# A recommendation tower on one core: layer 1 beside the next unit's first dots, layer 2 half a cycle on, the last unit's first tile in layer 1 ahead of the last rows

## The chip, the core and the metric

The kernel runs on one core of a Trainium2 chip. Time is device microseconds of one execution. The engines are TensorE (PE), VectorE (DVE), ScalarE (ACT), GpSimd (POOL) and SyncE (SP). Each works through its own list of instructions in order, and they wait for each other by semaphores only. DMAs are issued by SP, POOL and, at the end, ACT.

## What is computed

A batch of 2048 samples has one dense vector and 26 embeddings, gathered from 26 tables, all of 128 floats. The 351 dot products of all pairs of these 27 vectors, joined with the dense vector, go through three layers.

```python
e = jnp.stack([tbl_0[ids[:, 0]], ..., tbl_25[ids[:, 25]]], axis=1)   # 2048 x 26 x 128
T = concatenate([r_dense[:, None, :], e], axis=1)                   # 27 vectors of each sample
z = einsum('bnd,bmd->bnm', T, T)[:, iu0, iu1]                       # pairs n < m: 351
h = concatenate([z, r_dense], axis=1)                               # 479
h = maximum(h @ W_top1 + b_top1, 0.0)                               # 512
h = maximum(h @ W_top2 + b_top2, 0.0)                               # 256
y = h @ W_top3                                                      # 1
```

All of it is float32.

## The kernel before

The batch is cut into 16 tiles of 128 samples; two tiles (l = 0 and 1) are a unit, so there are 8 units u, and END is 7. Every sample needs its 27 vectors in `T`, with the 128 features on the partitions. They come in two ways.

*Rows.* 16 of the embeddings are gathered by GpSimd (`gather`, L420), one indirect DMA for each tile and table, into `rows[:, l]`. With the dense vector they make five rounds (`turn`, r = 0 to 4, with 3, 4, 4, 3 and 3 vectors). TensorE transposes a round into a bank of `look_ps` (`turn`, L743), and ScalarE copies it into `T` (`turn_out`, L600). `gather` of tile t waits until the same round of tile t - 2 has been turned.

*Lookups.* The 10 tables with 1000 rows are looked up by matrix products. VectorE compares ids with row numbers into `hot` (`compare`, L455), TensorE multiplies `hot` with the table, cut into a high part `tab_hi` and a low part `tab_lo` (`look`, L733), and ScalarE copies out (`look_out`, L588 or L592). The split of a table is VectorE's `split` (L440, L443) and ScalarE's `hi_out` (L568). Three tables, named WHOLE (1, 3 and 5), are split during unit 0's loop; their raw copies lie in the buffers that `w1` (chunks 0 and 1), `pairs` and `h1` use later, and the scratch of their split lies in `w2`. There are six lookup groups for a unit.

*Dots.* `products(u, l, b)` (L759) multiplies `T` with itself, 128 instructions for a tile. VectorE copies them to `gram` (`gram_out`, L479). For a unit SyncE stores `gram` in DRAM (`dots`, 4 DMAs, L337) and loads it back as `pairs`, in three chunks with pairs on the partitions (L342 and L343).

*Layers.* `layer1(u, ...)` (L779) has 16 products with 256 columns: for each of four output chunks f three chunks of `pairs` and one of the dense part. ScalarE's `h1_out` (L615) is bias and relu, eight instructions in two halves. `layer2(u)` (L789) has 8 products, VectorE's `y_out` (L489, L493) is the rest. The last unit goes tile by tile, with half the columns: `last_layer1(l)` (L800), `last_h1_out` (L622), `last_layer2` (L822), `last_y_out` (L498, L500). Its stores and loads are `shuffle_last` on SP and `last_store`, `last_load` on ACT.

The order on every engine is written out by hand. One turn of TensorE's loop for unit u is, in this order: turn(u,1,0), layer 2 of unit u-2, dots of tile (u,0), turn(u,1,1), lookup group 0 of unit u+1, turn(u,1,2), group 1, turn(u,1,3) and (u,1,4), group 2, half of layer 1 of unit u-1, turn(u+1,0,0), the other half, dots of tile (u,1), turn(u+1,0,1), group 3, turn(u+1,0,2) and (u+1,0,3), group 4, turn(u+1,0,4), group 5. At the end, after the loop: turn(END,1,0), layer 2 of unit 5, dots of (END,0), turn 1, layer 1 of unit 6 with turns 2 and 3 in between, turn 4, layer 2 of unit 6, dots of (END,1), then `last_layer1(0)`, `last_layer2(0)`, `last_layer1(1)`, `last_layer2(1)`. `look_ps` has four banks, taken in turn by turns and lookup groups.

SyncE's loop loads the dense vectors and the ids (`load_ids_near`) of later units, then calls `shuffle(u)`. In unit 0 it also loads the weights of layer 1, in many small pieces (L322): chunk 2 first, chunk 0 (9 pieces) when table 1 is split, chunk 1 (13 pieces) after the loads of the pairs, and then `w2`. All weights and biases count on one semaphore, `weights_landed`.

Of the kernel before, what the change touches and what calls it, by code (L numbers as in the profile page):

```python
# [63 lines left out]
def dlrm_tower(nc, r_dense, ids, tables, W1, b1, W2, b2, W3, out):  # L64
# [36 lines left out]
    WEIGHTS = 16 * (len(w1_pieces) + 5)  # L101
# [4 lines left out]
    with ExitStack() as ctx:  # L106
# [59 lines left out]
        weights_landed = sem("weights_landed")  # L166
# [92 lines left out]
        def l1_order(u):  # L259

            return (2, 3, 0, 1) if u == END - 1 else (0, 1, 2, 3)

        def last_l1(l, f):
            if l == 0:
                return look_ps[:, f // 2, f % 2 * P:(f % 2 + 1) * P]
            return [mlp_ps[:, 0, 0], mlp_ps[:, 1, 0], gram_ps[:, 0], gram_ps[:, 1]][f][:, 0:P]
# [31 lines left out]
        def _(sp):  # L299
# [19 lines left out]
            def load_pair_weights(c):  # L319
                for w_row, cnt, chunk, r, step in w1_pieces:  # L320
                    if chunk == c:
                        sp.dma_start(w1[r:r + step * (cnt - 1) + 1:step, c, :], W1[w_row:w_row + cnt, :]  # L322
                                     ).then_inc(weights_landed, 16)

            def load_small_weights():
                sp.dma_start(w1[:, PC, :], W1[PAIRS:PAIRS + D, :]).then_inc(weights_landed, 16)
                with nc.allow_non_contiguous_dma(reason="a few hundred words"):
                    sp.dma_start(bias1[:], b1.rearrange("(c p) -> p c", p=P)).then_inc(weights_landed, 16)
                sp.dma_start(w3[:], W3.rearrange("f o -> o f").to_broadcast([P, F2])).then_inc(weights_landed, 16)
                sp.dma_start(bias2[:], b2.rearrange("(o f) -> o f", o=1).to_broadcast([P, F2])).then_inc(weights_landed, 16)  # L330

            def shuffle(u):
# [3 lines left out]
                for j in range(NJ):  # L336
                    sp.dma_start(*dots_store(dots[u % 2], j, 0, 2 * NI)).then_inc(dots_stored, 16)  # L337
                if u >= 2:
# [36 lines left out]
            for u in range(END):  # L375
# [4 lines left out]
                if u == 0:  # L380
# [3 lines left out]
                    sp.wait_ge(lo_ready, split_count(WHOLE[1]))  # L384
                shuffle(u)
# [43 lines left out]
        def _(dve):  # L429
# [53 lines left out]
            def y_out(u):  # L483

                if u == 0:
                    dve.wait_ge(weights_landed, WEIGHTS)
# [43 lines left out]
            for u in range(END):  # L530
# [3 lines left out]
                if u > 1:  # L534
                    y_out(u - 2)
# [6 lines left out]
                gram_out(u, 1)  # L542
                if u == 0:
# [12 lines left out]
            y_out(END - 2)  # L556
            dense_out(END, 1)
            gram_out(END, 1)
            y_out(END - 1)
# [4 lines left out]
        def _(act):  # L564
# [39 lines left out]
            def h1_out(u, half):  # L604
                if u == 0 and half == 0:
                    act.wait_ge(weights_landed, WEIGHTS)
# [3 lines left out]
                for f in l1_order(u)[half * F1C // 2:(half + 1) * F1C // 2]:  # L610
# [7 lines left out]
            def last_h1_out(l):  # L618
                for step in range(F1C if l else F1C // 2):
                    act.wait_ge(l1_done, 2 * END + 2 * l + step + 1)  # L620
                    for f in ([step] if l else [2 * step, 2 * step + 1]):
# [45 lines left out]
            for u in range(END):  # L667
                turn_out(u, 1, 0)
                turn_out(u, 1, 1)
                look_out(u + 1, 0)  # L670
# [8 lines left out]
                if u > 0:  # L679
                    h1_out(u - 1, 0)  # L680
                    h1_out(u - 1, 1)
# [3 lines left out]
                look_out(u + 1, 3)  # L685
                if u == 0:
                    hi_out(WHOLE[1])
                turn_out(u + 1, 0, 2)
# [8 lines left out]
            h1_out(END - 1, 0)  # L697
            turn_out(END, 1, 2)
            turn_out(END, 1, 3)
            h1_out(END - 1, 1)  # L700
            turn_out(END, 1, 4)
            last_store(range(NJ // 2, NJ))
            last_h1_out(0)
# [4 lines left out]
        def _(pe):  # L708
# [54 lines left out]
            def layer1(u, first, end):  # L763
                for i in range(first, end):
                    f, c = l1_order(u)[i // (PC + 1)], i % (PC + 1)
                    if i == 0:
                        if u == 0:
                            pe.wait_ge(weights_landed, WEIGHTS)
# [160 lines left out]
```

## Time and profile before

| | us |
|---|---|
| median of 3 runs | 368.12 |
| lowest, highest | 367.59, 368.23 |
| the profiled execution | 367.97 |
| its span, from the first to the last instruction | 366.2 |

| engine | busy us | share of the span |
|---|---|---|
| TensorE, matmul | 343.0 | 94% |
| TensorE, weight load | 320.5 | 88% |
| VectorE | 221.5 | 60% |
| ScalarE | 172.3 | 47% |
| GpSimd | 256.3 | 70% |

### The profile page before, as it was taken

The numbers are of one execution on the slowest core, as the hardware profiler recorded it, in microseconds if no ns is written. First come the engines' busy times: TensorE is split into PE (matmuls) and PEld (weight loads), VectorE is DVE, ScalarE is ACT, GpSimd is POOL, SyncE is SP. The second block draws the span as 40 slices with busy tenths as digits, with TensorE's granted clock in tenths as the row PEclk, the third lists the DMA queues.
The fourth block names the chain that finished last, engine by engine and source line by source line (L and its number), as shares of the span: only waits on it lengthen the run. The fifth ranks groups of instructions, "written<-read, shape, count | busy, mean of one in ns | idle before, by whom it ended". The sixth has DMA issues, their size and how long they took to land.

```text
span 366.2 us, 9895 instructions
## 1 busy us (share of the span) xinstructions
PE 343.0 (94%) x4042; PEld 320.5 (88%) x4042; DVE 221.5 (60%) x786; ACT 172.3 (47%) x220; POOL 256.3 (70%) x263
## 2 busy tenths in 40 slices
PE   3997899879699999999999999999999999999976
PEld 2887798769689999999989999999989998999766
DVE  3989968886436677375936576466936484613231
ACT  5266738543356345561556244563556253344211
POOL 6787777777777777777777777777777777775000
PEclk9999999999899999999999999999999999999998
DMA  7996232355325622255215622363225322454030
GB/s 208 268 260 179 62 124 77 86 146 166 104 56 119 177 62 57 70 132 162 59 52 134 167 63 58 78 154 124 60 59 134 98 59 52 99 133 86 21 57 6
DMA packets 45878, 39.07 MB, mean 107 GB/s; under 512 B 32930, under 2 KB 39113, under 8 KB 45834
## 3 DMA queue, kind: packets, MB, share of 16 engines
q1 hardware_dynamic: 36014, 21.40, 22.1%
q0 software_dynamic: 8192, 16.79, 17.7%
q8 instruction: 32, 0.52, 0.6%
q10 hardware_dynamic: 1628, 0.25, 0.5%
q14 instruction: 12, 0.10, 0.1%
HBM read 32.40 MB, written 6.02 MB: 105 GB/s over the span
## 4 chain that ended last, share of the span: by engine, by line
PE 82%; DVE 4%; POOL 4%; DMA 4%; issue 3%; ACT 1%; ACTq 0%; SPq 0%; DVEq 0%
PE look_ps L733 35%; PE gram_ps L759 14%; PE mlp_ps L779 13%; PE look_ps L743 7%; PE mlp_ps L789 7%; POOL rows L420 4%; PE look_ps L724 4%; DVE hot L455 3%; DMA rows<-in_tbl_dram,ids_all 1%; DMA dots_last<-gram 1%; DMA ids_all<-in_ids_dram 1%; DMA pairs<-dots_last 1%; PE mlp_ps L800 1%; PE gram_ps L800 1%; PE look_ps L822 1%
## 5 line engine op out<-in xcount | busy, mean ns | idle before, releaser
L420 POOL DMA_INDIRECT rows<-in_tbl_dram,ids_all x240 | 237.6, 990 | 73.2 <-issue 71.0
L455 DVE TENSOR_SCALAR hot<-ids_near 125x256 fp32r<-125x256 f16 x640 | 148.4, 302 | 43.2 <-PE look_ps L733 34.5
L733 PE MATMUL look_ps<-hot,tab_hi 125*128 125x256 f32 x616 | 155.5, 292 | 5.8 <-ACT tab_hi L568 2.9
L733 PE MATMUL look_ps<-hot,tab_lo 125*128 125x256 f32 x616 | 151.1, 284 | 0.0
L733 PEld LDWEIGHTS look_ps<-hot,tab_hi 125*128 125x128 f32 x616 | 118.6, 192 | 7.4 <-issue 5.3
L600 ACT COPY T<-look_ps 128x384 f32<-128x384 f32 (+1 forms) x80 | 85.4, 1113 | 71.6 <-PE look_ps L743 71.6
L733 PEld LDWEIGHTS look_ps<-hot,tab_lo 125*128 125x128 f32 x616 | 118.8, 193 | 0.1
L479 DVE COPY gram<-gram_ps 128x432 f32<-128x432 f32 x64 | 38.8, 607 | 68.9 <-PE gram_ps L759 56.2
L592 ACT COPY T<-look_ps 128x512 f32<-128x512 f32 x32 | 38.6, 1206 | 75.3 <-PE look_ps L733 75.3
L759 PEld LDWEIGHTS gram_ps<-T 128*54 128x54 f32 x2048 | 53.9, 130 | 8.5 <-issue 4.5
L759 PE MATMUL gram_ps<-T 128*54 128x54 f32 x2048 | 57.4, 214 | 2.1 <-DVE gram L479 1.0
L743 PE MATMUL look_ps<-ident,rows 128*128 128x128 f32 x272 | 41.5, 276 | 3.2 <-DMA rows<-in_tbl_dram,ids_all 1.8
L779 PE MATMUL mlp_ps<-pairs,w 117*128 117x256 f32 x168 | 40.9, 379 | 0.0
L743 PEld LDWEIGHTS look_ps<-ident,rows 128*128 128x128 f32 x272 | 31.1, 141 | 5.6 <-DMA rows<-in_tbl_dram,ids_all 2.1
L779 PEld LDWEIGHTS mlp_ps<-pairs,w 117*128 117x128 f32 x168 | 30.7, 189 | 3.7
L789 PE MATMUL mlp_ps<-w,h 128*128 128x256 f32 x112 | 25.4, 380 | 0.9 <-ACT h L615 0.9
L789 PEld LDWEIGHTS mlp_ps<-w,h 128*128 128x128 f32 x112 | 20.7, 190 | 3.7 <-ACT h L615 1.1
L615 ACT ACTIVATE h<-mlp_ps,bias 128x128 f32<-128x128 f32 x56 | 16.0, 382 | 12.9 <-PE mlp_ps L779 12.9
L420 POOL DMA_INDIRECT rows<-in_tbl_dram,ids_first x16 | 17.9, 1117 | 5.8 <-issue 4.6
L577 ACT ACTIVATE ids_near<-ids_near,minus_row 125x2560 f16<-125x2560 f16 x7 | 17.0, 2435 | 0.7 <-DMA ids_near<-ids_rows 0.7
L779 PE MATMUL mlp_ps<-dense,w 128*128 128x256 f32 x56 | 16.7, 379 | 0.0
L588 ACT COPY T<-look_ps 128x256 f32<-128x256 f32 x16 | 11.5, 719 | 5.8 <-PE look_ps L733 5.8
(72 smaller groups left out, 133.6 us busy)
## 6 DMA issues: line engine op xcount, KB each, us to landing
dots<-gram SPq DMA_DIRECT2D x28, 182.2 KB
ids_near<-ids_rows SPq DMA_DIRECT2D x7, 640.0 KB, 6.3
rows<-in_tbl_dram,ids_all POOLq DMA_INDIRECT x240, 2.6
T<-in_tbl_dram SPq DMA_DIRECT2D x5, 448.0 KB
pairs<-dots SPq DMA_DIRECT2D x14, 117.0 KB
rows<-in_r_dense_dram SPq DMA_DIRECT2D x16, 64.0 KB
gram<-in_tbl_dram SPq DMA_DIRECT2D x2, 448.0 KB
pairs<-dots SPq DMA_DIRECT2D x7, 104.0 KB
```

Of the source, the lines that this page charges most:

```text
L420: pool.indirect_dma_start(rows[:, t % 2, place[n], :], None, tables[n - 1], bass.IndirectOffsetOnAxis(ap=index[:, n - 1:n].bitcast(U32), a ...
L455: eq = nc.vector.tensor_scalar(hot[:VP, at % 2, c], ids_near[:VP, u % 2, k], float(c), None, ALU.is_equal)
L479: nc.vector.tensor_copy(gram[:, :, :, first:first + PER], gram_ps[:, b % 2, 0:2 * PER * NV].rearrange("p (i s n) -> p s n i", s=2, n=NV)). ...
L577: nc.scalar.activation(ids_near[:VP, u % 2], ids_near[:VP, u % 2], ACT.Identity, bias=minus_row[:VP]).then_inc(ids_relative, K)
L592: nc.scalar.copy(T_unit(u)[:, :, :, n0:n1 + 1:n1 - n0].rearrange("p l q n -> p n l q"), src.rearrange("p (n l q) -> p n l q", n=2, l=2)).t ...
L600: nc.scalar.copy(T_tile(u, l)[:, :, n:n + cnt].rearrange("p q n -> p n q"), look_ps[:, bank_of(("turn", u, l, r)), 0:cnt * P].rearrange("p ...
L615: relu = nc.scalar.activation(by_sample[:, g], by_pair[:, g], ACT.Relu, bias=bias1[:, f:f + 1])
L733: mm = pe.matmul(dst, w[:VP, k, c], hot[:VP, slot, c], start=(c == 0 and half == 0), stop=(c == CH - 1 and half == 1))
L743: mm = pe.transpose(look_ps[:, bank, i * P:(i + 1) * P], rows[:, l, place[n], :], ident[:])
L759: mm = pe.matmul(gram_ps[64 * g:64 * g + 2 * NV, b % 2, at:at + 2 * NV], src[:, g, i], src[:, g, i], start=True, stop=True)
L779: mm = pe.matmul(mlp_ps[:, f * 2 // F1C, f % 2], w1[:kk, c, f * P:(f + 1) * P], rhs, start=(c == 0), stop=(c == PC))
L789: mm = pe.matmul(mlp_ps[:, 0, l], h1[:, c, l * P:(l + 1) * P], w2[:, c], start=(c == 0), stop=(c == F1C - 1))
```

## The change

SyncE's `shuffle(u)` is cut into `store_dots(u)` and `load_pairs(u)`. In unit 0 weight chunk 1 is issued right behind chunk 0, ahead of the stores, and `w2` between the stores and the loads of the pairs. `weights_landed` becomes three semaphores: `w1_landed`, `w2_landed` and `small_landed` (dense part of W1, biases, W3).

On TensorE layer 1 is cut into `layer1_dense(u)`, the dense products of output chunks 0 and 2, and `layer1_pairs(u)`, the other 14. In the loop `layer1_dense(u-1)` stands ahead of the dots of tile (u,0), where layer 2 of unit u-2 stood, and `layer1_pairs(u-1)` behind turn(u,1,1). `layer2(u-1)` stands where the second half of layer 1 stood, behind turn(u+1,0,0). At the end `layer2(END-1)` and then `last_layer1(0)` stand ahead of turn(END,1,4) and of the last dots, and `last_layer1(0)` writes to one bank of `mlp_ps`. ScalarE's `h1_out` goes behind turn_out(u,1,1), `hi_out(3)` goes ahead of look_out(1,3), and `last_h1_out(0)` goes ahead of `last_store`. VectorE's `y_out(u-1)` goes behind `gram_out(u,1)`, where `y_out(u-2)` stood further ahead.

```diff
@@ SyncE
+                    load_pair_weights(1)
+                store_dots(u)
                 if u == 0:
-                    load_pair_weights(1)
                     sp.wait_ge(hi_ready, K)
                     sp.wait_ge(lo_ready, K)
-                    sp.dma_start(w2[:], W2.rearrange("(c p) f -> p c f", p=P)).then_inc(weights_landed, 16)
+                    sp.dma_start(w2[:], W2.rearrange("(c p) f -> p c f", p=P)).then_inc(w2_landed, 16)
+                load_pairs(u)
...
@@ VectorE
-                if u > 1:
-                    y_out(u - 2)
                 dense_out(u, 1)
...
                 gram_out(u, 1)
+                if u > 0:
+                    y_out(u - 1)
...
@@ ScalarE
                 turn_out(u, 1, 1)
+                if u > 0:
+                    h1_out(u - 1, 0)
+                    h1_out(u - 1, 1)
                 look_out(u + 1, 0)
...
                 turn_out(u + 1, 0, 1)
+                if u == 0:
+                    hi_out(WHOLE[1])
                 look_out(u + 1, 3)
-                if u == 0:
-                    hi_out(WHOLE[1])
...
             turn_out(END, 1, 4)
+            last_h1_out(0)
             last_store(range(NJ // 2, NJ))
-            last_h1_out(0)
...
@@ TensorE
+            def layer1_dense(u):
+
+                if u == 0:
+                    pe.wait_ge(small_landed, SMALL_LANDED)
+                pe.wait_ge(dense_ready, 2 * u + 2)
+                if u > 0:
+
+                    pe.wait_ge(y_ready, 2 * u)
+                    pe.wait_ge(h1_ready, F1C * u)
+                for f in range(0, F1C, 2):
+                    layer1_begin(u, f)
+
+            def layer1_pairs(u):
+                if u == 0:
+                    pe.wait_ge(w1_landed, W1_LANDED)
+                pe.wait_ge(shuffled[u % 2], SHUFFLED * (u // 2 + 1))
...
                 turn(u, 1, 0)
-                if u > 1:
-                    layer2(u - 2)
+                if u > 0:
+                    layer1_dense(u - 1)
                 for b in range(BLOCKS):
                     products(u, 0, b)
                 turn(u, 1, 1)
+                if u > 0:
+                    layer1_pairs(u - 1)
...
-                if u > 0:
-                    layer1(u - 1, 0, 8)
                 turn(u + 1, 0, 0)
                 if u > 0:
-                    layer1(u - 1, 8, 16)
+                    layer2(u - 1)
...
             turn(END, 1, 3)
...
+            layer2(END - 1)
+            last_layer1(0)
             turn(END, 1, 4)
-            layer2(END - 1)
             for b in range(BLOCKS):
                 products(END, 1, b)
-            last_layer1(0)
             last_layer2(0)
```

## Rows read from the trace of the kernel before

**Rows 1.** The page's part 1: busy us, share of the span, instructions.

```profile
PE 343.0 (94%) x4042; PEld 320.5 (88%) x4042; DVE 221.5 (60%) x786; ACT 172.3 (47%) x220; POOL 256.3 (70%) x263
```

**Rows 2.** Timeline of GpSimd, the last gather: start us, us, what, idle before.

```profile
335.02 0.94 POOL L420 DMA_INDIRECT rows<-in_tbl_dram,ids_all  x1 [0.31 <-issue]
```

**Rows 3.** Chain of waits in unit 2's loop: start us, us, what.

```profile
152.25 0.58 PE look_ps L743 x4
152.84 3.84 PE look_ps L733 x32
...
161.92 3.46 PE mlp_ps L789 x16
```

**Rows 4.** Timeline of TensorE, start of unit 1, rows with idle time before them.

```profile
71.68 0.36 PE L733 MATMUL look_ps<-hot,tab_hi 125*128 125x256 f32 x1 [1.56 <-ACT tab_hi L568]
...
75.42 0.35 PE L733 MATMUL look_ps<-hot,tab_hi 125*128 125x256 f32 x1 [1.27 <-DVE hot L455]
...
82.98 0.66 PE L743 MATMUL look_ps<-ident,rows 128*128 128x128 f32 x4 [0.43 <-DMA rows<-in_tbl_dram,ids_all]
```

**Rows 5.** Chain of waits, unit 1, ahead of and behind its last turn.

```profile
88.77 4.35 DMA rows<-in_tbl_dram,ids_all
...
93.66 1.46 issue
...
95.72 5.25 PE look_ps L733 x32
```

**Rows 6.** Windows: A:B, length, busy PE PEld DVE ACT POOL, granted clock, DMA share, GB/s.

```profile
95.10:101.00 5.90, 5.88 (x36) 5.90 (x37) 2.11 (x9) 0.92 (x1) 4.51 (x5) 0.71 0.24 65
...
358.20:361.40 3.20, 3.20 (x17) 3.20 (x16) 0.00 (x0) 1.15 (x4) 0.00 (x0) 0.51 0.00 0
```

**Rows 7.** Timeline of VectorE around the split of the last table.

```profile
68.89 1.82 DVE L455 TENSOR_SCALAR hot<-ids_near 125x256 fp32r<-125x256 f16 x8
71.63 0.69 DVE L440 TENSOR_SCALAR w<-h 125x1024 int32<-125x1024 int32 x1 [0.92 <-ACT tab_hi L568]
```

**Rows 8.** Timeline of SyncE's queue, DMA issues: start us, us of issuing, line.

```profile
60.64 3.80 SPq L322 DMA_DIRECT2D w<-in_W_top_dram  x9
69.00 5.43 SPq L337 DMA_DIRECT2D dots<-gram  x4
77.38 2.24 SPq L342 DMA_DIRECT2D pairs<-dots  x3
79.66 0.48 SPq L343 DMA_DIRECT2D pairs<-dots  x1
80.18 6.78 SPq L322 DMA_DIRECT2D w<-in_W_top_dram  x13
...
164.71 0.48 SPq L343 DMA_DIRECT2D pairs<-dots  x1
```

**Rows 9.** Chain of waits from the last unit's first dots to the end.

```profile
324.34 3.46 PE mlp_ps L789 x16
...
337.87 1.75 PE mlp_ps L779 x8
...
340.84 3.72 PE mlp_ps L789 x16
344.56 3.49 PE gram_ps L759 x128
...
354.50 2.44 DMA pairs<-dots_last
...
361.34 1.96 PE look_ps L822 x8
```

**Rows 10.** Timeline of VectorE behind the second tile's dots, unit 2.

```profile
154.86 3.89 DVE L455 TENSOR_SCALAR hot<-ids_near 125x256 fp32r<-125x256 f16 x16 [1.95 <-PE look_ps L733]
```

**Rows 11.** Timeline of TensorE behind the last dots, the start of last_layer2(0).

```profile
351.63 0.69 PE L822 MATMUL look_ps<-w,h 128*128 128x256 f32 x2
```

**Rows 12.** Timeline of ScalarE, a turn's copy near the end.

```profile
337.91 0.91 ACT L600 COPY T<-look_ps 128x384 f32<-128x384 f32 x1 [0.27 <-PE look_ps L743]
```

More of the change, by code:

```diff
@@ L555, in _ @@
             gram_out(END, 0)
-            y_out(END - 2)
+            y_out(END - 1)
             dense_out(END, 1)
             gram_out(END, 1)
-            y_out(END - 1)
             last_y_out(0)
@@ L609, in h1_out @@
                     act.wait_ge(l2_done, u)
-                for f in l1_order(u)[half * F1C // 2:(half + 1) * F1C // 2]:
+                for f in range(half * F1C // 2, (half + 1) * F1C // 2):
                     by_sample = h1[:, f].rearrange("p (l g i s) -> p g s l i", l=2, g=2, s=2)
@@ L618, in last_h1_out @@
             def last_h1_out(l):
-                for step in range(F1C if l else F1C // 2):
-                    act.wait_ge(l1_done, 2 * END + 2 * l + step + 1)
-                    for f in ([step] if l else [2 * step, 2 * step + 1]):
+                for step in range(F1C if l else 1):
+                    act.wait_ge(l1_done, 2 * END + l + step + 1)
+                    for f in ([step] if l else range(F1C)):
                         nc.scalar.activation(h1[:, f, l * P:(l + 1) * P].rearrange("p (g i s) -> p g s i", g=2, s=2),
@@ L684, in _ @@
                 turn_out(u + 1, 0, 1)
-                look_out(u + 1, 3)
                 if u == 0:
                     hi_out(WHOLE[1])
+                look_out(u + 1, 3)
                 turn_out(u + 1, 0, 2)
@@ L761, in products, with layer1_begin @@
                 mm.then_inc(gram_done, 1)
[L763 to L766, printed above, removed]
-                        if u == 0:
-                            pe.wait_ge(weights_landed, WEIGHTS)
-                        pe.wait_ge(shuffled[u % 2], SHUFFLED * (u // 2 + 1))
-                        pe.wait_ge(dense_ready, 2 * u + 2)
-                    if u > 0 and c == 0 and f == 0:
-                        pe.wait_ge(y_ready, 2 * u)
-                    if u > 0 and c == 0 and f == 2:
-                        pe.wait_ge(h1_ready, F1C * u)
-                    kk = P if c == PC else KP
-                    rhs = dense[:, u % 2] if c == PC else pairs[:kk, u % 2, c]
-                    mm = pe.matmul(mlp_ps[:, f * 2 // F1C, f % 2], w1[:kk, c, f * P:(f + 1) * P], rhs,
-                                   start=(c == 0), stop=(c == PC))
-                    if c == PC and f % 2 == 1:
+            def layer1_begin(u, f):
+                pe.matmul(mlp_ps[:, f * 2 // F1C, f % 2], w1[:, PC, f * P:(f + 1) * P], dense[:, u % 2],
+                          start=True, stop=False)
+            def layer1_dense(u):
[11 more added lines that the diff above has]
+                pe.wait_ge(shuffled[u % 2], SHUFFLED * (u // 2 + 1))
+                for f in range(F1C):
+                    if f % 2 == 1:
+                        layer1_begin(u, f)
+                    for c in range(PC):
+                        mm = pe.matmul(mlp_ps[:, f * 2 // F1C, f % 2], w1[:KP, c, f * P:(f + 1) * P],
+                                       pairs[:KP, u % 2, c], start=False, stop=(c == PC - 1))
+                    if f % 2 == 1:
                         mm.then_inc(l1_done, 1)
             def layer2(u):
+                if u == 0:
+                    pe.wait_ge(w2_landed, W2_LANDED)
                 pe.wait_ge(h1_ready, F1C * (u + 1))
```

45 lines of the change are left out of this document (20 added, 25 removed).

## The prediction

> **What bounds the kernel now.** I read five views. The page's busy shares come first [rows 1]: TensorE is busy 343.0 of 366.2 us and GpSimd, with its gathers, 256.3 us. The latter figure understates GpSimd, because between two gathers it always pauses 0.30 us. Its last gather starts at 335.02 and ends at 335.96 [rows 2], 256 gathers of some 1.3 us end to end. So two engines run through side by side with no reserve to speak of. The chain of waits says which of them ends last. From 95.7 us to 339.6 us it stays on TensorE without a hole, with a period of 40.6 us per unit. [Rows 3] are three pieces of it: the dots of the second tile of unit 2 end at 152.25, a lookup group of 32 instructions takes 3.84, and the 8 products of layer 2 at 161.92 take 3.46; layer 1 has 16 products of the same width. In that stretch an order on TensorE costs nothing and brings nothing as long as no wait appears or goes. What an order can change lies in two places: the start of unit 1 (70 to 101 us), where TensorE waits, and the end (after 324 us).
>
> In the start, the timeline of TensorE shows waits of 1.56 us for ScalarE's `tab_hi`, of 1.27 us for VectorE's `hot` and of 0.43 us for gathered rows [rows 4]; the chain then has 1.46 us more ahead of the last `turn`, and after that 32 lookup instructions take 5.25 us [rows 5] instead of 3.84. The granted clock tells why: 0.71 over 95.1 to 101 and 0.51 over 358.2 to 361.4 [rows 6], which is a stretch at the 1.2 GHz level (full busy time; 5.9 x 0.29 / 0.5 = 3.4 us of it in the first), each time after TensorE had been largely idle. Such a stretch under full work costs half its length, 1.7 us.
>
> **The start, step by step.** Three edits meet here.
>
> (a) ScalarE makes `hi_out` of whole table 3 ahead of `look_out(1, 3)`. VectorE's `hot` for that table ends at 68.89 + 1.82 = 70.71, and its next split began only at 71.63 because it waited 0.92 us for `tab_hi` [rows 7]. With the copy made first, lookup group 4 starts at 70.8 in place of 71.68 and the chain behind (split, `hot`, lookup group 5 at 75.42) comes 0.9 us earlier: `turn(1,1,0)` ends at about 76.8 in place of 77.7.
>
> (b) SyncE issues the 13 pieces of weight chunk 1 ahead of the stores of the dots and the big `w2` load ahead of the loads of the pairs. The old order is in [rows 8]: 9 pieces until 60.64 + 3.80 = 64.44, stores 69.00 to 74.43, pair loads 77.38 to 80.14, 13 pieces in 6.78 us after that. The new one: pieces 64.4 to 71.2, stores 71.2 to 76.7, `w2` one issue (about 0.5), landed stores 2.95 us after their last issue, as before (74.43 to 77.38), so 79.6; pair loads issued 79.6 to 82.4. A pair load took 2.44 us from issue to the matmul that uses it [rows 9]; the last one, issued at 81.9, is there at 84.4 on quiet queues. With `w2` and gathers in flight I take 85.0. The bounds are 84.0 and 86.3 (4.35 us, the gathered rows that came late in the same traffic [rows 5]).
>
> (c) TensorE now has 2 dense products (2 of the 8 in 3.46 us [rows 3], 0.87) ahead of the dots of unit 1, and 14 products (6.05 us) right behind `turn(1,1,1)`. Dots at 77.7 + 3.5 = 81.2; that turn waited for its rows until 82.98 [rows 4], which land perhaps 0.5 earlier with less traffic; it ends at 83.1. The products wait for the pairs until 85.0: a new wait of 1.9 us, bounds 0.9 and 3.2. Behind it, on TensorE's queue, stand everything of units 1 and 2, so nothing covers it. They end at 91.05. Then three lookup groups (3 x 3.84), the turns (1.43) and layer 2 (3.46) make 16.4, so the dots of the second tile start at 107.5 against 108.2 before, with layer 2 of unit 0 already done. The old waits at 93 and 95 us are gone, since the rows are long there. But TensorE is idle from 81.2 with one 0.6 us turn between until 85.0, 3.2 us in all, which is like the idle ahead of 95 us and more than the 2.5 us ahead of 358 us [rows 6, 9]. I take it that the 1.2 GHz stretch comes again, at the same 1.7 us: 109.1, that is +0.9. Without it -0.8.
>
> **The steady units.** Layer 1 moves 11 to 14 us earlier, layer 2 half a unit. Their instructions are the same 16 + 8 products, so TensorE's period stays. VectorE's `y_out` (three short operations) goes between the last copy of the dots and a `hot` that waits for a lookup anyway: VectorE idles there for 1.95 us in unit 2 [rows 10], and in the others as long. I take it as hidden; without that hole it would delay lookup group 4 by at most its own length. ScalarE's eight relus now stand ahead of a `look_out` whose lookup takes 3.84 us; they take 2.3. What gets near is the pairs: the dots of a unit end, and layer 1 of it starts 9.67 us (152.25 to 161.92) + 0.87 + 3.5 + 0.59 = 14.6 us later, at 166.9 in unit 2. The last pair load is issued at 164.71 and is there at 164.71 + 2.44 = 167.15, or 0.4 later with traffic [rows 3, 8, 9]. Unit 2 has the latest of these loads (its stores took longest), unit 5 the next; the others issue about a microsecond sooner. I take 0.3 us in all, bounds 0 and 1.5. GpSimd sees all this only through `turned` of two tiles back, some 30 us of reserve, and keeps its pace. The turns of the second and third row rounds come later, that of round 1 earlier by 2.6 us; its rows have been there long enough for that in the trace.
>
> **The end.** Before, from 324.34: layer 2, dots, turn, layer 1 with turns, a wait of 340.84 - 339.62 = 1.22 us for the relus, layer 2 for 3.72, dots at 344.56 [rows 9]. After: 2 products 0.87, dots 3.53, turn 0.59, 14 products 6.05 (335.38), two turns beside the relus' 1.22 (336.6), layer 2 3.72 (340.3), then the 16 half-width products of `last_layer1(0)`. Before, they ran at 348.05 to 351.63 [rows 11], in the shadow of the store and load of the last dots (until 356.94), for nothing. Now they lie ahead of the last turn and cost 3.46: 343.8. Their pairs are not late: dots at 328.74 instead of 331.33, so landed some 2.6 earlier, at about 339.5. Then the turn 0.33, and ScalarE's copy of it 0.91 [rows 12], which layer 2 used to cover and nothing does now: dots at 345.1 against 344.56, +0.55. The last rows are no excuse to hide the 3.46 behind: they are gathered by 335.96 [rows 2] and there by about 338.5, while TensorE now arrives at 343.8.
>
> The tail after these dots (copy, store, load, 12 products, layer 2, `last_y_out`) has the same steps. I take it as before, 21.6 us, half-clock stretch included.
>
> **Sum.** 366.2 + 0.9 + 0.3 + 0.55 = 367.95 as span; on the profiled execution's 367.97 that is 369.7. The median is 0.15 above that execution: 369.9.
>
> **The rivals.** (1) The clock holds at 85 us, because a turn falls into the idle time: -1.7, 368.2. For: a wait of 1.56 and one of 1.27 us at 70 to 75 us left the clock at 1.00. Against: the idle here is 3.2 us in 3.8.
> (2) Faster. The pairs of unit 0 are there when TensorE arrives, so that neither the 1.9 us wait nor the slow stretch exists: 369.9 - 3.6 = 366.3. It decides if the last pair load lands by 83.1 us. For it: the old store took from 69.00 and nothing says that the 13 weight pieces hold it up for all of 2.2 us. Against: the issue order and 0.5 us per issue [rows 8].
> (3) Slower still. TensorE now runs out of work ahead of the tail: with `last_layer1(0)` gone from there it is idle from about 351.5 to 357.5, against 2.5 us before. The 1.2 GHz level then holds from the first of the 12 products. At 2.4 GHz these would take 2.6 us and layer 2 1.73; before, they took 4.4 (356.94 to 361.34) and 1.96 [rows 9]. All at half, 5.2 + 3.5 = 8.7, is +2.4: 372.3. The Trainium skill, TensorE: Matmul & The Clock Gate, section Part 1: The HAM clock gate, says that the throttled level is the default and only activity releases it; by that rule a longer idle ahead of the tail is never free. The trace of before agrees as far as it goes (0.51 after 2.5 us idle). How late in the tail the level comes back no row here shows.
> (4) The order has no effect beyond the two ends and the gains and losses there cancel: the start brings 0.8 (rival 1 in small) and the end takes it: 368.1.
>
> **Chances.** Forecast 0.40 (own range 369.0 to 370.8), rival 1 0.24, rival 2 0.15, rival 3 0.12, rival 4 0.09. A difference of 0.2% (0.74 us) is about what a measurement of this kernel can tell from none. Slower (above 368.9): nearly all of the forecast and rival 3, and a sixth of rival 1: 0.55. Faster (under 367.4): rival 2 and some of rival 1: 0.20. Same: 0.25. The range goes from rival 2 with little to spare to just short of rival 3: 366.5 to 371.9.
>
> **What the new profile would show.** Right: a wait of TensorE for the DMA of the pairs of unit 0 at 83 to 85 us; a granted clock of 0.5 soon after; the second dots of unit 1 at 109 us; a pair wait of some tenths near 167; `last_layer1(0)` at 340 to 344 and the last dots at about 346.7. Wrong: dots of unit 1 before 107 us (rival 2), no clock under 1.00 before the tail (rival 1), the 12 last products over 5 us (rival 3), or repeated pair waits of a microsecond in the steady units, which would put the time above the range.

## The result: 1 to 2% slower, and the profile after

| | before | after |
|---|---|---|
| median, us | 368.12 (7 runs, 367.56 to 369.40) | 373.46 (7 runs, 370.47 to 379.87) |
| the profiled execution, us | 367.97 | 377.54 |
| its span, us | 366.2 | 375.7 |

The ratio is 1.0108 with a 95% interval of 1.0078 to 1.0139. Ratios, here and below, leave out executions over 1.5% above the fastest of their kernel (of the changed kernel the three longest, 376.3 to 379.9 us, with the profiled one among them); medians leave out none. On a second chip the same kernel gave 376.45 us against 367.51, ratio 1.0226 (1.0189 to 1.0264), and the profile taken there (span 376.2) has waits of the same kinds. That one, at 377.99 us, is the longest of its six. So I read both profiles, take no size from one alone, and keep in mind that both show more than the median execution lost (9.5 us of span in the first, where the medians differ by 5.3). The forecast was 369.9 us with a range of 366.5 to 371.9. Its sign held, its size and range did not.

The page after, parts 1, 2 (granted clock) and 4:

```profile
PE 345.9 (92%) x4042; PEld 322.3 (86%) x4042; DVE 222.7 (59%) x786; ACT 171.4 (46%) x220; POOL 258.9 (69%) x263
...
PEclk9999999996999999999999999999999999999988
...
PE 73%; DMA 10%; SPq 8%; ACT 4%; DVE 2%; issue 1%; ACTq 0%; DVEq 0%
```

TensorE has the same 4042 matmul instructions as in [rows 1] and 2.9 us more busy time; the same instructions last longer where the clock is low. New in the chain of waits are 8% on SyncE's queue and 10% on DMAs: the chain now runs through the stores and loads of the dots, where before it stayed on TensorE from unit 1 to the last unit. Here are its pieces at the start (start us, us, what):

```profile
84.50 3.42 DMA pairs<-dots
88.06 2.90 PE mlp_ps L788 x6
...
95.78 1.30 PE mlp_ps L788 x6
...
113.50 3.49 PE gram_ps L760 x128
```

The first products with pairs (line 788) start at 88.06, when the last pair load of unit 0 has landed. The first group of six takes 2.90 us and the last 1.30. The dots of the second tile of unit 1 start at 113.50. The same chain further on, in the loop's unit 2 (pairs of unit 1), in its unit 5 (pairs of unit 4), and at the end:

```profile
128.33 4.28 DMA pairs<-dots
132.65 1.56 PE mlp_ps L788 x6
...
251.50 3.99 DMA pairs<-dots
...
319.54 3.46 PE gram_ps L760 x128
...
349.09 3.57 PE mlp_ps L811 x32
...
353.02 0.92 ACT T L601
...
353.99 3.56 PE gram_ps L760 x128
...
363.93 2.40 DMA pairs<-dots_last
```

Two rows of the kernel before are wanted beside these, the dots of the second tile of unit 1 and of unit 6:

```profile
108.22 3.46 PE gram_ps L759 x128
...
311.20 1.90 PE gram_ps L759 x65
```

With the last dots at 344.56 [rows 9] they cut the loss of the two profiled executions into parts. The second column is the trace after, the third that from the second chip (113.41, 318.36 and 354.50 there):

| | before | after | after, second chip |
|---|---|---|---|
| start of the dots of tile (1,1) | 108.22 | +5.3 | +5.2 |
| from there to those of (6,1) | 202.98 | +3.1 | +2.0 |
| from there to the last dots | 33.36 | +1.1 | +2.8 |
| from there to the end of the span | 21.6 | +0.1 | +0.1 |

### The profile page after: what moved, and what is told of

The parts are those of the page before. It is cut to its first block, busy times and chain, and to the rows that moved or that the text cites. A ratio compares the mean times of both kernels' runs of the same rounds, so it can differ in the third digit from the quotient of the medians.

```text
span 375.7 us, 9896 instructions
## 1 busy us (share of the span) xinstructions
PE 345.9 (92%) x4042; PEld 322.3 (86%) x4042; DVE 222.7 (59%) x786; ACT 171.4 (46%) x220; POOL 258.9 (69%) x263
## 4 chain that ended last, share of the span: by engine, by line
PE 73%; DMA 10%; SPq 8%; ACT 4%; DVE 2%; issue 1%; ACTq 0%; DVEq 0%
PE look_ps L734 31%; PE gram_ps L760 11%; PE mlp_ps L788 11%; PE mlp_ps L800 7%; PE look_ps L744 6%; DMA dots<-gram 4%; PE look_ps L725 4%; DMA pairs<-dots 3%; SPq L337 3%; PE mlp_ps L765 3%; SPq L322 3%; SPq L344 2%; DMA w<-in_tbl_dram 2%; PE mlp_ps L811 2%; DVE gram L481 1%
## 5 line engine op out<-in xcount | busy, mean ns | idle before, releaser
L422 POOL DMA_INDIRECT rows<-in_tbl_dram,ids_all x240 | 240.2, 1001 | 73.2 <-issue 69.2
L734 PEld LDWEIGHTS look_ps<-hot,tab_hi 125*128 125x128 f32 x616 | 117.2, 190 | 6.8 <-ACT T L589 2.3
L734 PEld LDWEIGHTS look_ps<-hot,tab_lo 125*128 125x128 f32 x616 | 117.5, 191 | 0.2
L788 PE MATMUL mlp_ps<-pairs,w 117*128 117x256 f32 x168 | 42.4, 397 | 4.5 <-DMA pairs<-dots 4.5
L788 PEld LDWEIGHTS mlp_ps<-pairs,w 117*128 117x128 f32 x168 | 32.9, 199 | 10.0 <-issue 3.2
```

The source lines that it names most:

```text
L422: pool.indirect_dma_start(rows[:, t % 2, place[n], :], None, tables[n - 1], bass.IndirectOffsetOnAxis(ap=index[:, n - 1:n].bitcast(U32), a ...
L734: mm = pe.matmul(dst, w[:VP, k, c], hot[:VP, slot, c], start=(c == 0 and half == 0), stop=(c == CH - 1 and half == 1))
L788: mm = pe.matmul(mlp_ps[:, f * 2 // F1C, f % 2], w1[:KP, c, f * P:(f + 1) * P], pairs[:KP, u % 2, c], start=False, stop=(c == PC - 1))
```

## What was open, and two ways of reading it

Theory A, which is the prediction's with larger sizes: TensorE waits for the pairs of unit 0 and loses its clock by that, meets late pairs again in some later units, and has `last_layer1(0)` uncovered at the end. Theory C is its rival: the new sequence of blocks costs something in itself, so that moving the wait away brings nothing back. Inside theory A it was open whether the idle time makes the clock fall, and what makes the pairs late.

## Experiments: taking the parts back

Every ratio is to the kernel before, run beside it on the same chip. The first run is the changed kernel itself (`f1_after`).

> The changed kernel on another chip than the runs before it, where every kernel took some 515 us or more because TensorE waited for its own instructions. Here I expect about 368 us for the kernel before and a ratio of 1.006 to 1.014. Theory A: wait for the pairs of unit 0 of 2 to 3.5 us, a clock of 0.5 behind it, waits of a microsecond in all for later pairs, last dots 9 us later than in the kernel before or less if the clock holds.

It gave 376.45 us, 1.0226, more than the 1.006 to 1.014 expected. Its wait for the pairs of unit 0 is 2.3 us, those of later units 1.6 us. The waits of TensorE in that trace (engine, line, what it waited for: us in total, times, longest):

```profile
PE mlp_ps L811 <- DMA pairs<-dots_last: 6.1, 1, 6.1
PE mlp_ps L788 <- DMA pairs<-dots: 3.9, 3, 2.3
```

**The products with pairs one lookup group back.**

```diff
                 turn(u, 1, 1)
-                if u > 0:
-                    layer1_pairs(u - 1)
                 look(u + 1, 0)
+                if u > 0:
+                    layer1_pairs(u - 1)
```

ScalarE's two `h1_out` go behind `look_out(u + 1, 0)` in the same way.

> The 14 products with pairs one lookup group (3.84 us) further back. Theory A: no wait for pairs from unit 0 to 5, the slow stretch at 88 us gone: 3 to 6 us less than the changed kernel, ratio to before 0.997 to 1.003. Theory C (it is the sequence of blocks on TensorE and not the waits): ratio as that of the changed kernel.

369.96 us, 1.0070 (1.0044 to 1.0096), 6.5 us under the changed kernel on the same chip. In its trace TensorE has no wait at line 788 at all, and the chain reads:

```profile
106.70 3.46 PE gram_ps L760 x128
...
310.62 3.46 PE gram_ps L760 x128
...
344.67 3.56 PE gram_ps L760 x128
```

The dots of tile (1,1) are 1.5 us earlier than before the change, not 5 later, and from there to (6,1) it takes 203.9 us where the changed kernel took 206.0 and, on this chip, 205.0. The same instructions in almost the same sequence, 3.84 us later in each unit, give 6.5 us back: theory C falls. The ratio stays above the 0.997 to 1.003 that was expected. The profiled execution, at 368.11 us the fastest of the six, is level with the trace of before: 1.5 us less at the start, 0.9 more up to the dots of (6,1), 0.7 more from there to the last dots. What makes the median 2.4 us longer than the kernel before (369.96 against 367.51) no trace shows.

**Unit 0 alone.** The same edit for u = 1 only, that is for the pairs of unit 0.

> The changed kernel with the pairs' products of unit 0 alone one lookup group back, on such a chip. Theory A: the loss at the start (2.3 to 3.0 us of wait, 3.0 of slow clock) goes, the waits of the later units stay: 369 to 372 us, ratio 1.005 to 1.012, between the changed kernel (1.023) and the one with all units moved (1.007).

370.36 us, 1.0076 (1.0048 to 1.0103). Against the 1.0226 of the changed kernel, which ran on another chip, the start alone is worth 1.5 points, some 5.5 us; in the trace the dots of (1,1) come at 106.53, 6.9 us earlier. One wait for pairs (0.8 us, in the loop's unit 5) is left. The ratio can't be told from that of the kernel with all units moved, so the later units' waits aren't a fixed charge that comes on top.

**The last tile back.**

```diff
             layer2(END - 1)
-            last_layer1(0)
             turn(END, 1, 4)
             for b in range(BLOCKS):
                 products(END, 1, b)
+            last_layer1(0)
```

with `last_h1_out(0)` behind `last_store` again.

> last_layer1(0) and its relus behind the last dots. Theory A: 3.5 us (1.0%) less than the changed kernel; the wait for the last pairs after the last dots falls from 6 us to 2.5. If the tail gives it back, under 1 us less.

1.0002 (0.9970 to 1.0033) against 1.0226: 8 us, where 3.5 were expected. The twelve executions lie between 364.9 and 373.7 us; their median is 370.2, 6.3 us less than the changed kernel's. The trace (371.25 us) shows the expected part: from the dots of (6,1), at 316.61, to the last dots, at 347.81, it is 31.2 us against 34.5 and 36.1 in the two traces of the changed kernel, while the wait for the last pairs falls from 6.1 to 1.8 us.

```profile
PE mlp_ps L788 <- DMA pairs<-dots: 3.3, 3, 1.8
PE look_ps L744 <- DMA rows<-in_tbl_dram,ids_all: 2.1, 1, 2.1
PE mlp_ps L811 <- DMA pairs<-dots_last: 1.8, 1, 1.8
```

The rest is the start, in which the two kernels are the same: here the wait for the pairs of unit 0 was 1.8 us and the clock stayed at 1.00, so that the dots of (1,1) came at 109.46. That is 4 us earlier than in the traces of the changed kernel, and it does not belong to the edit. The clock did fall at the end: the last 12 products take 4.58 us, though TensorE waited only 1.8 us ahead of them.

```profile
360.26 0.71 PE mlp_ps L811 x4
...
361.59 0.85 PE mlp_ps L811 x4
...
363.30 0.85 PE mlp_ps L811 x4
```

The next run gives the edit's share without late pairs.

**Both edits.**

> Both edits at once: the products with pairs one lookup group back and last_layer1(0) behind the last dots. Theory A: the parts add up, 3.5 us below the first alone; with the earlier tab_hi and no rows waited for at 93 us this is 2 to 5 us below the kernel before, ratio 0.987 to 0.995. If the gathers are the limit (their last rows land at 337.4 us of the span), no gain against the kernel before.

364.89 us, 0.9926 (0.9901 to 0.9951): 2.6 us faster than the kernel before and 11.6 faster than the changed kernel. Against the kernel with the first edit alone it is 5.1 us. 3.6 of these lie ahead of the last dots (341.53 - 311.05 = 30.5 us from the dots of (6,1), instead of 34.05). 1.6 lie behind them: the last 12 products take 2.94 us (354.04 to 356.98) instead of 4.58 (357.06 to 361.64), at a granted clock of 1.00. `last_layer1(0)` in front of the wait doesn't explain that by itself: the run before this one has the same order there, a wait of 1.8 us instead of 1.9, and its clock fell. Why it held here is open. It is the best version of this study, and it holds the rest of the change (split semaphores, weights and `hi_out` earlier, layer 2 half a cycle on). Its timeline near the end, the last gather of GpSimd and the chain:

```profile
335.77 0.94 POOL L422 DMA_INDIRECT rows<-in_tbl_dram,ids_all  x1 [0.30 <-issue]
```

```profile
340.19 0.34 PE look_ps L744 x3
...
340.56 0.93 ACT T L601
```

The last rows are gathered at 336.7, 0.8 us from the end in [rows 2]: GpSimd didn't move. TensorE takes the last turn at 340.19. The reserve of the gathers is down to about 2 us (a gather takes 2.5 us from its issue to its landing by the page of this run). In the chain that ended last GpSimd's gathers now have 19%, against 4% in the kernel before, and TensorE waits for rows three times, 2.7 us in all. So I expect that orders of TensorE alone can bring little more; no run tried. The expectation allowed 2 to 5 us.

## Experiments: the clock

**Work in the wait at the start.** Four products without use (0.43 us each, into a half bank that layer 1 overwrites) and `layer1_dense(0)` behind them fill the wait.

```diff
-                if u > 0:
+                if u > 1:
                     layer1_dense(u - 1)
...
                 turn(u, 1, 1)
+                if u == 1:
+                    for _ in range(4):
+                        pe.matmul(mlp_ps[:, 1, 1], ident[:], w1[:, PC, 0:Q], start=True, stop=True)
+                    layer1_dense(u - 1)
                 if u > 0:
                     layer1_pairs(u - 1)
```

> The changed kernel with TensorE kept at work while it waits for the pairs of unit 0: behind turn(1,1,1) four products into an unused half bank (0.43 us each, their result is overwritten), and layer1_dense(0) behind them. The wait itself stays. Theory A (half of the loss at the start is the 1.2 GHz stretch that the idle time brings): granted clock 1.00 over 84 to 97 us, the 14 products take 6.1 in place of 9.0 us, 3 us (0.8%) less than the changed kernel. If the stretch does not come from the idle time, the clock falls all the same and the time stays or grows by up to 0.8 us.

Windows of the changed kernel (first fence, the trace of the first chip) and of this one (second): A:B, length, busy PE PEld DVE ACT POOL, granted clock, DMA share, GB/s.

```profile
84.00:87.50 3.50, 0.87 (x14) 0.50 (x8) 0.91 (x2) 1.17 (x1) 2.72 (x3) 0.90 0.67 195
87.50:97.00 9.50, 8.95 (x29) 7.47 (x30) 0.00 (x0) 1.15 (x4) 7.06 (x9) 0.68 0.40 113
```

```profile
84.00:87.50 3.50, 3.50 (x18) 3.08 (x17) 0.00 (x0) 1.17 (x1) 2.77 (x3) 1.00 0.83 267
87.50:97.00 9.50, 9.50 (x63) 8.86 (x62) 2.24 (x10) 2.73 (x9) 7.19 (x8) 1.00 0.20 62
```

In the changed kernel 0.10 x 3.5 + 0.32 x 9.5 = 3.4 us of full clock are missing, which is 6.8 us at 1.2 GHz, twice the stretch in [rows 6]; in the kernel with the filling none is. The dots of (1,1) come at 109.03 instead of 113.50. One trace alone would prove little, since the clock also held at the start in two traces without filling (109.46 above, and one below). But all six executions with the filling have a mean clock of 0.991, which in the traces goes with a start at full clock and a slow stretch at the end; of the 19 executions of the changed kernel and of the one with `w2` moved (below) only four reach it, the others have 0.982 or 0.986. So the idle time does bring the slow clock. The time, however, didn't follow: 375.28 us, 1.0192 (1.0146 to 1.0238), no better than the run beside it (below, 1.0181) in whose trace the clock fell. The later waits for pairs in this trace add up to more than in the two of the changed kernel:

```profile
PE mlp_ps L788 <- DMA pairs<-dots: 3.0, 4, 1.1
```

3.0 us in four later units, against 1.5 and 1.6 us. I can't say whether the filling causes that, and leave it open.

**Work in the wait at the end**, twelve such products behind `last_layer2(0)` in the changed kernel, and five in the kernel before:

```diff
             last_layer2(0)
+            for _ in range(12):
+                pe.matmul(look_ps[:, 0, 0:Q], ident[:], w1[:, PC, 0:Q], start=True, stop=True)
```

> The changed kernel with twelve products of 0.43 us into an unused bank behind last_layer2(0), in the 6.0 us that TensorE waits for the last pairs. Theory A: the last 12 products run at 2.4 GHz, 2.6 us in place of 4.6, 2 us (0.5%) less than the changed kernel. Otherwise the same time.

> The kernel before with five such products in its 2.5 us wait for the last pairs. Theory A: the last 12 products take 2.6 us in place of 4.4: 1.5 to 1.8 us less than the kernel before, ratio 0.995 to 0.996. Otherwise the same.

The first and the last group of the last 12 products of the changed kernel (first fence; only the last two of its six groups run at full clock) and of the one with the filling (second; all six do, the granted clock there is 1.00), from the chains:

```profile
366.37 1.22 PE mlp_ps L811 x4
...
370.62 0.45 PE gram_ps L811 x4
```

```profile
369.45 0.71 PE mlp_ps L811 x4
...
371.95 0.45 PE gram_ps L811 x4
```

They take 2.95 us instead of 4.69. In the kernel before the same filling takes them from 4.36 [rows 9] to 2.94 us (357.77 to 360.71). The times agree only loosely: 366.96 us against 367.74, ratio 0.9975 (0.9949 to 1.0002), so half of the expected 1.5 us, and not clear of none. The changed kernel with the filling gave 376.3 us as median of nine executions and a ratio of 1.0079 (1.0038 to 1.0121); the nine lie between 368.3 and 378.9 us, too far apart to see 2 us. What these runs show is the mechanism in the traces, not its worth.

## Experiments: what makes the pairs late

**`w2` behind the pairs.**

```diff
-                    sp.dma_start(w2[:], ...).then_inc(w2_landed, 16)
                 load_pairs(u)
+                if u == 0:
+                    sp.dma_start(w2[:], ...).then_inc(w2_landed, 16)
```

> The changed kernel with the 512 KB load of w2 issued behind the loads of the pairs of unit 0, not ahead of them. Theory A with my price of the wait: the w2 load holds the pairs up by its share of the queues: the wait for the pairs of unit 0 falls from 2.3 to 3.0 us to 1 to 2 us and the slow stretch may go with it: 1 to 4 us less than the changed kernel. If the stores set the landing alone (SyncE waits for them anyway), the wait stays within 0.3 us.

374.84 us, 1.0181 (1.0136 to 1.0226); the wait was 2.2 us, inside the 1.8 to 3.0 that the changed start shows in four other traces. The chain says why:

```profile
76.02 5.09 DMA dots<-gram
...
83.86 2.85 DMA pairs<-dots
...
86.85 2.90 PE mlp_ps L789 x6
```

SyncE waits for the stores until 81.1 without `w2` in front, and until 80.5 to 82.0 with it in the four other traces. The last pair load still needs 2.85 us; in the four it was 2.95 to 4.14. So `w2` doesn't set the start of the loads; whether it costs the last one some tenths, one trace can't tell.

**Nothing behind the pairs.**

```diff
                 load_pairs(u)
+                if u < END - 1:
+                    sp.wait_ge(shuffled[u % 2], SHUFFLED * (u // 2 + 1))
```

> The changed kernel, but SyncE waits until the pairs of a unit have landed before it issues the next dense vectors and ids_near, on a chip where the kernel before takes 368 us. Theory D (the ids_near load right behind the pair loads holds them up): the time from the issue of the last pair load to the first product falls from 3.4 to 4.3 us to 2.4 to 3.0 us where TensorE waits for it, the waits of units 1 to 5 go, 1.5 to 3 us less than the changed kernel. Theory E (traffic that is always there): landing and waits as before, no change of the time.

375.14 us, 1.0190 (1.0146 to 1.0235), and its chain has

```profile
205.38 4.44 DMA pairs<-dots
...
330.44 4.06 DMA pairs<-dots
```

The last pair load takes 4.1 to 4.4 us with no `ids_near` behind it, as in the changed kernel (4.28 and 3.99) and as in unit 6 (the row at 330.44), where there is none to load. Theory D falls. What is left of the traffic in the loop are the gathers and the pair loads themselves; that one of them holds the landing up follows by exclusion only, and wasn't tried by itself.

This run has a second lesson. In its trace the wait for the pairs of unit 0 is 0.84 us, the clock stays at 1.00 and the dots of (1,1) come at 108.85, some 4.6 us earlier than in the changed kernel. Its ratio can't be told from that of the changed kernel all the same, as with the filling above. From the dots of (1,1) to the last dots it is 241.9 us in both, against 236.3 before the change and 240.5 and 241.1 in the two traces of the changed kernel. The spans of these two traces (373.3 and 373.2 us) are 2.4 to 3.0 us shorter than the 375.7 and 376.2 there, but those belong to long executions of their kernel. So even with a good start this order stays some 7 us behind the kernel before.

**Six runs on a chip where TensorE stood still for other reasons.** Two sets of runs fell on a chip where the kernel before took 515 and 528 us. In the trace of `e1_after_again` TensorE stands 65.2 us ahead of the dots alone (76 times) in what the profile calls `issue`, time in which it waited for nothing that the profile shows; in the trace of before `issue` is 2.6 us in all. That its own instructions came late is my reading of this, not shown. The mean granted clock was 0.871.

```profile
PE gram_ps L760 <- issue: 65.2, 76, 6.8
```

> The changed kernel once more, to have a second trace of it. Theory A (TensorE waits about 3 us for the pairs of unit 0 and then runs at 1.2 GHz, waits about a microsecond in all for the pairs of units 2 and 5, and has last_layer1(0) uncovered at the end): ratio 1.008 to 1.014, the wait for pairs at 85 to 88 us between 2 and 3.5 us, a clock of 0.5 behind it. Theory B (the first trace caught an accident of the tables' landing at the start): the wait at 85 us is gone or under 1 us, ratio under 1.006.

> The 14 products with pairs move one lookup group (3.84 us) further back, in every unit but the last; nothing else. Theory A: all waits for pairs go, with them the slow stretch at 88 us; against the changed kernel -3.0 (wait) -3 (clock) -1.4 (other units) in the profiled run, against the kernel before within 0.3%: about 368 us. Theory C (the new order loses by how the blocks follow on each other on TensorE, not by waits for pairs): no change against the changed kernel, ratio to before stays at 1.01.

> Only last_layer1(0) and its relus go back behind the last dots, where the store and the load of the last dots cover them. Theory A: 3.5 us less than the changed kernel, 368 to 369 us, as the 16 products were uncovered ahead of the last dots. Rival: the relus and layer 2 behind the last dots then get in the way and the tail gives it back, or the gathered rows were the limit there: under 1 us less.

> As the run that moves the products with pairs one lookup group back, but for unit 0 alone. Theory A: the wait of 3 us and the slow stretch go, the waits of units 1 to 6 stay: 4 to 6 us less than the changed kernel in the trace, about 1.4 us more than the kernel with all units moved. If unit 0 is not where the time is lost, under 1 us less than the changed kernel.

The four gave 1.0230, 1.0223, 1.0126 and 1.0228 with intervals of some 0.5 points to either side. They are, in this order, the changed kernel, all units moved, the last tile back and unit 0 alone. Putting the last tile back brought 5 us there too. Moving the products with pairs brought nothing: with TensorE this late the pairs are there (one wait, 1.1 us, in the changed kernel, and one of 1.3 us with the products moved), so nothing was to be had from it.

> The changed kernel, but SyncE waits until the pairs of a unit have landed before it issues the next dense vectors and ids_near (640 KB). In the traces of the changed kernel the last pair load takes 3.4 to 4.3 us from its issue to the first product, where the quiet end of the kernel shows 2.4. Theory D (the ids_near load right behind them holds them up): that time falls to 2.4 to 3.0 us in units 0 to 5, the waits for pairs of units 1 to 5 go, 1.5 to 3 us less than the changed kernel. Theory E (the gathers and the descriptors of the pairs themselves do it): 3.0 to 4.3 us as before and waits as before, no change of the time.

> The changed kernel with the pairs' products of unit 0 alone one lookup group back, on a chip where TensorE gets its instructions in time. Theory A: the loss at the start (2.3 to 3.0 us of wait, 3.0 of slow clock) goes, the waits of the later units stay: 369 to 372 us, ratio 1.005 to 1.012, between the changed kernel (1.023) and the one with all units moved (1.007).

These two gave 1.0146 (1.0077 to 1.0215) and 1.0101 (1.0012 to 1.0190) and tell nothing on their question; they were run again as above.

## Why the prediction was right in its sign and wrong in its size

The step that failed is the price of a pair load's landing in the steady units: 2.44 us plus 0.4 for traffic, 0.3 us of waiting in all. Where TensorE waited, the landing took 3.6 to 4.8 us. The term for the start was too small as well, mostly because the loads of unit 0 were issued later than forecast and the slow stretch was twice as long. Each step in turn:

(a) *`tab_hi` earlier.* Right. In the trace of `f4_both` lookup groups 4 and 5 start at 70.92 and 74.51, forecast 70.8 and 74.5; the waits ahead of them are 0.70 and 1.12 us instead of the 1.56 and 1.27 of [rows 4].

(b) *The pairs of unit 0.* The order of steps was right, the landing was not. SyncE's queue after (start us, us of issuing):

```profile
62.11 11.03 SPq L322 DMA_DIRECT2D w<-in_W_top_dram  x22
73.18 5.31 SPq L337 DMA_DIRECT2D dots<-gram  x4
78.61 0.88 SPq L391 DMA_DIRECT2D w<-in_W_top_dram  x1
81.73 2.73 SPq L344 DMA_DIRECT2D pairs<-dots  x3
84.50 0.49 SPq L345 DMA_DIRECT2D pairs<-dots  x1
```

All is 1.5 to 2.6 us behind the forecast; 1 us of it is the start of the kernel, which in this execution was late before the change had done anything (first dots at 44.29 instead of 43.30; in `f2_pairs_later` and `f4_both`, with the same start, 42.94). The last load was issued at 84.50 instead of 81.9 and took 3.6 us to its first product, where the forecast had 3.1. So the pairs came at 88.06, forecast 85.0 with an upper bound of 86.3; in the other five traces with this start or nearly this start it was 86.2 to 87.7, above the bound in all but one. The wait became 3.0 us, and 2.3, 2.8, 2.2, 1.8 and 0.8 in the others, forecast 1.9 with bounds of 0.9 and 3.2. That it stayed inside its bounds in five of six is partly luck: TensorE came late too.

(c) *The clock.* The mechanism was right: idle time, then 1.2 GHz. The price was one stretch as in [rows 6], 1.7 us. It was 9.0 us for the 14 products instead of 6.05, so 3.0 us. The prediction took the length of the one stretch that the trace before shows at the start as the length of all. A second trace of the same start, that of `g3_before_fill_end`, has twice as much of it (0.16 x 9.5 + 0.12 x 16 = 3.4 us of full clock missing):

```profile
87.50:97.00 9.50, 6.36 (x45) 5.95 (x44) 5.51 (x24) 4.91 (x5) 7.19 (x8) 0.84 0.60 183
97.00:113.00 16.00, 16.00 (x195) 14.72 (x194) 5.96 (x21) 6.48 (x11) 12.21 (x13) 0.88 0.20 58
```

Of the Trainium skill's rule (TensorE: Matmul & The Clock Gate, section Part 1: The HAM clock gate) that activity releases the throttled level, the two traces of the changed kernel show as much as that the level held for 6.8 us with TensorE at work for most of them. Rival 1, that the clock holds, came true where the wait was 1.8 us or less (`f3_last_tile_back`, `i1_loads_alone`) and never in the four with 2.2 us or more. That is no threshold: at the end of `f3_last_tile_back` the clock fell behind a wait of 1.81 us, and at the end of `f4_both` it held behind one of 1.86.

*The start in sum*: forecast +0.9, measured +5.3. The missing 4.4 us are 3.1 of later pairs and 1.3 of clock. Of the 3.1, 2.6 are the later issue of the last load (1.0 of that the late start) and 0.5 its landing. `turn(1,1,0)` also had to wait 1.1 us for rows that the forecast saw landed in time; that lies ahead of the wait for the pairs, which ended last, and so costs nothing of its own. From the end of the 14 products to the dots it is 16.4 us, as forecast. In the two traces where the clock held without filling, the start lost 1.2 and 0.6 us, close to the forecast, but without the slow stretch that the forecast had in it.

*The steady units*: this is the step that failed. The forecast priced the landing of a pair load in the loop with the 2.44 us of [rows 9], a row of the kernel's quiet end, added 0.4, and found 0.3 us for all units, at most 1.5. Where TensorE waited for it in the loop, the last pair load took 3.6 to 4.8 us to land. TensorE arrives 14.6 us after the end of the dots, and with the last load issued 11.0 to 12.2 us after it the late pairs come 15.1 to 16.8 us after it: every unit is near to waiting or waits. Some wait: 1.0 and 0.4 us in one trace, 1.3 and 0.3 in the other. Around each, the first six products take 1.56 us in place of 1.30, and small waits of 0.2 to 0.5 us for VectorE's copies appear in some dots. The forecast also had no term for the pairs of unit 6, which came late by 0.7 to 1.5 us in five of the six traces that keep the changed order up to the last dots (the two of the changed kernel, the two with filling, those with `w2` behind the pairs and with nothing behind the pairs). From the dots of (1,1) to the last dots these six took 4.2 to 7.6 us more than before, where steady units and end together were forecast at 0.85; 1.5 to 4.0 us of it are waits for pairs, and with all units moved, without such a wait, 1.6 us more remain. This holds for the traces with a good start as for the others. The trace before could not show the landing, because nobody waited for it. The bound had to be taken from the busy row, the 4.35 us of [rows 5], which the same prediction used for unit 0.

*The end*: right but for late pairs. Forecast +0.55; `f2_pairs_later`, free of late pairs, has 344.67 - 310.62 = 34.05 against 33.36, +0.7. The changed kernel's +2.8 on the second chip holds 1.3 us for the pairs of unit 6 beside it; in the +1.1 of the first trace they are in time, and 0.3 us is a wait for VectorE's copy. `last_layer1(0)` takes 3.57 us (349.09), forecast 3.46, and the copy 0.92. The last rows were no cover for it, as forecast.

*The tail*: +0.1. Rival 3 feared 2.4 us from a clock that is low all through. TensorE is idle for 6.1 us there instead of 2.5, but the 12 products took 4.7 us against 4.4, and layer 2 1.80 against 1.96: before, too, most of them had run at 1.2 GHz. Rival 2 (pairs early, faster) didn't happen in any of the six executions profiled with this start or nearly this start. Rival 4 can't be told from the others by a trace and its 368.1 us didn't come.

## What to carry to other kernels

A DMA whose landing nobody waits for has no price in a trace; when an edit brings the consumer near, take its landing from the busiest row of the same kind of stretch, not from a quiet one, and count how far every repetition is from waiting. Look for work that already sits in a wait, as `last_layer1(0)` did: it was free there, and moved ahead of the last dots it cost 3.6 us. And when an order fails by a microsecond or two of waiting, move the consumer by one block before giving the order up: here that, with the last tile put back, turned 1 to 2% slower into 0.7% faster.

## What the runs showed of the hardware

- The clock fell to 1.2 GHz at the start in four of four executions in which TensorE waited 2.2 to 3.0 us for the pairs behind one short turn, and stayed in two with waits of 0.8 and 1.8 us. The slow stretch was 6.8 us each time. With the start of before it was 3.4 us in one trace and 6.8 in another. The wait alone doesn't decide: at the end of the kernel the clock fell behind a wait of 1.81 us in one trace and held behind 1.86 us in another, with the same order.
- The mean clock of an execution explains its time only in part. Of the first seven executions of the changed kernel the two at 0.991 took 370.5 and 372.2 us, that at 0.986 took 371.0, the four at 0.982 took 373.5 to 379.9. But the six with the filling at the start, all at 0.991, lie between 371.7 and 377.1 us.
- The orders with late pairs also spread more. The changed kernel's executions lie 9.4 and 4.3 us apart on two chips and those with the last tile put back 8.9 us, but those with all units moved only 2.7 us and those with both edits 1.7 us.
- GpSimd issued 256 gathers at some 1.3 us each and ended at 336 to 339 us in twelve traces from the chips where the kernel before takes 368 us, whether the span was 361.6 or 377.1 us. No order on TensorE tried here moved that end by more than 3 us.
- On the chip where TensorE stood in `issue`, the kernel took 40% longer with the same instructions, and the worth of an edit changed: putting the last tile back kept its 5 us, removing the waits for pairs was worth nothing.
